# Sorting edges inside a graph network kernel: two products a bucket, names split into a power of two and a share, one-hots in batches of four

## The reference

```python
src, dst = ...                         # 41250 edges, both ends and self loops
xs = x[:, :C] @ W_in2f_s; xv = x[:, C:] @ W_in2f_v     # the table, from layernorm(x)
sj, vj = xs[idx_j], xv[idx_j]          # gathered by edge
W = (shifted_softplus(f_ij @ Wf1 + bf1) @ Wf2 + bf2) * rcut_ij[:, None]
x_ij = products of sj, vj, W and the edge's direction
agg = jax.ops.segment_sum(x_ij, idx_i, num_segments=n)
...
x = x + graph_layer(layernorm(x), ...)
x = x + experts(layernorm(x), ...)     # top-k tokens of 8 experts
```

## Time and profile before

| | us |
|---|---|
| median of 3 runs | 1451.07 (1449.11 to 1451.34) |
| the profiled execution | 1450.21 |
| its span | 1448.2 |
| last product of a column ends, about | 166.7 |
| first product of the loop starts | 178.4 |

### The profile page before, as it was taken

How to read it: one execution, slowest core, us unless ns; L and a number is a source line. 1 busy time by engine, 2 the same in 40 slices (tenths; PEclk the granted TensorE clock), 3 DMA queues, 4 the chain that set the end, 5 groups by cost and what they waited for, 6 DMA issues and landing times. The chain is left out here.

```text
span 1448.2 us, 26881 instructions
## 1 busy us (share of the span) xinstructions
PE 1336.5 (92%) x7095; PEld 786.7 (54%) x7095; DVE 1034.6 (71%) x2533; ACT 830.7 (57%) x2124; POOL 791.2 (55%) x834
## 2 busy tenths in 40 slices
PE   6888699999999999999999999999972699999997
PEld 1463356555555555555655555555561455555553
DVE  6998679989999899899999999999776311111110
ACT  5589777777777777777777777777551011111111
POOL 3147577777777777777777777777300122222211
PEclk7699889999999999999999999999995799999998
DMA  7135044444444444445443444434452155555521
GB/s 245 74 131 161 4 112 113 125 127 124 128 124 113 123 129 123 129 123 143 124 113 110 112 112 111 113 109 115 68 186 72 58 163 163 162 162 157 149 37 18
DMA packets 65872, 172.46 MB, mean 119 GB/s; under 512 B 14260, under 2 KB 22820, under 8 KB 65191
## 3 DMA queue, kind: packets, MB, share of 16 engines
q0 software_dynamic: 43424, 105.53, 28.2%
q1 hardware_dynamic: 22398, 66.38, 13.5%
HBM read 148.53 MB, written 18.08 MB: 115 GB/s over the span
## 5 line engine op out<-in xcount | busy, mean ns | idle before, releaser
L1114 PE MATMUL PS<-prod,oneh 128*64 128x256 f32 x2052 | 469.5, 382 | 6.4 <-DVE region_s L929 3.6
L562 POOL DMA_INDIRECT recs<-rec_d,inv_i x342 | 323.5, 946 | 117.2 <-issue 85.8
L573 POOL DMA_INDIRECT gath<-table_d,recs x342 | 324.1, 948 | 106.2 <-issue 77.1
L1114 PEld LDWEIGHTS PS<-prod,oneh 128*64 128x64 f32 x2052 | 268.5, 137 | 202.2 <-issue 80.3
L697 ACT ACTIVATE oneh<-oneh,recs 128x64 f32<-128x64 f32 x1026 | 282.2, 337 | 151.9 <-DVE oneh L906 150.6
L1107 PE MATMUL PS<-prod,oneh 128*64 128x256 f32 x1368 | 356.0, 392 | 0.0
L1095 PE MATMUL PS<-wf_sb,h_t 128*128 128x512 f32 x684 | 333.0, 609 | 2.9 <-DVE h_t L892 2.9
L917 DVE TENSOR_TENSOR prod<-PS,gath 128x768 f32<-128x768 f32 x342 | 323.3, 945 | 0.0
L929 DVE TENSOR_TENSOR region_s<-region_s,PS 128x512 f32 x342 | 231.7, 677 | 22.5 <-issue 16.7
L704 ACT COPY PS<-c_rep 128x512 f32<-128x512 f32 x338 | 190.7, 584 | 74.9 <-DVE prod L917 73.5
L1095 PEld LDWEIGHTS PS<-wf_sb,h_t 128*128 128x128 f32 x684 | 117.1, 191 | 118.9 <-issue 115.6
(11 more groups left out here) (262 smaller groups left out, 1520.8 us busy)
## 6 DMA issues: line engine op xcount, KB each, us to landing
region_r<-wu SPq DMA_DIRECT2D x16, 512.0 KB, 4.1
region_r<-wd SPq DMA_DIRECT2D x16, 512.0 KB, 5.6
region_u<-wu SPq DMA_DIRECT2D x16, 512.0 KB, 4.2
region_u<-wd SPq DMA_DIRECT2D x16, 512.0 KB, 5.4
recs<-rec_d,inv_i POOLq DMA_INDIRECT x342
gath<-table_d,recs POOLq DMA_INDIRECT x342, 3.3
region_u<-rec_in SPq DMA_DIRECT2D x1, 5168.0 KB, 21.7
rec_d<-region_u SPq DMA_DIRECT2D x1, 5168.0 KB
```

What stands on the lines that cost most here:

```text
L562: nc.gpsimd.indirect_dma_start(out=recs[:, q % RING, k, :], out_offset=None, in_=rec_d, in_offset=bass.IndirectOffsetOnAxis(ap=inv_i[:, t: ...
L573: nc.gpsimd.indirect_dma_start(out=gath[:, t % GRING, :], out_offset=None, in_=table_d, in_offset=bass.IndirectOffsetOnAxis(ap=recs[:, q % ...
L1114: return nc.tensor.matmul(to, oneh[:, slot, 1 + i, :], prod[:, slot, P_Q:P_B + i + 1:1 + i, :], start=i == 0, stop=i == 2, skip_group_chec ...
```

## The change

- `rec_in` is loaded ahead of the weights and x, x last. POOL does `lengths` before `weights`; ACT takes that root ahead of its work on x, and DVE the reciprocal in the middle of the buckets.
- The two halves of a column's start lie in one operand of 52 rows (`column_parts`), so a bucket takes two products. `row_of` gets a second copy of its rows, by a second ACT instruction.
- A name is a power of two that depends on the column, put on the tile one-hot as a constant (`weight(n)`), times a share that depends on the row alone, put on the slot one-hot (`share`). So ACT's Relu has the same operands for every column, and does four at once, 128x512, into a ring of its own of 16 (`scalar_oh`). The distances' ring holds two batches. There are 152 such columns (38 batches): four in nine up to column 143 and five in nine behind it (`LATE`). POOL has 61, from column 48 on.
- `node_variance` stands behind column 18, `node_scales` behind column 24, and two batches' distances and one Relu ahead of the normalising.
- The seeds stand behind the last column.
- `read_names` runs over the first 24 tiles and then over the rest, and POOL's gather of tile 24 waits for the second.

```diff
+LATE = 144
+BATCH = 4
+SCALAR_RING = 16
...
 def by_scalar(n):
-    return n >= ALONE and n % 9 % 2 == 1
+    return n >= ALONE and n % 9 in ((1, 3, 5, 7) if n < LATE else (1, 3, 5, 7, 8))
 def by_pool(n):
-    return n >= 8 * BESIDE and n % 9 in (4, 8)
+    return n >= 2 * ALONE and n % 9 in (0, 4)
...
-FAR = 4
+FAR = 2
+def weight(n):
+    return math.ldexp(-1.0 if n >= HALF else 1.0, LEAST + n % HALF - 127)
+FIRST = 24
...
                 sp.dma_start(src_i, src).then_inc(s_src, 16)
-                for cut in CUTS:
-                    sp.dma_start(x_sb[cut], x.rearrange("(p t) h -> p t h", t=BLOCKS)[cut]).then_inc(s_x, 16)
+                sp.dma_start(unsorted, rec_in).then_inc(s_edges, 16)
...
                     sp.dma_start(to, of).then_inc(s_small, 16)
-                sp.dma_start(unsorted, rec_in).then_inc(s_edges, 16)
+                for cut in CUTS:
+                    sp.dma_start(x_sb[cut], x.rearrange("(p t) h -> p t h", t=BLOCKS)[cut]).then_inc(s_x, 16)
...
-                    pool.wait_ge(s_rt, 2)
+                    pool.wait_ge(s_rt, 1)
...
+                lengths()
                 weights()
-                lengths()
                 directions()
                 constants()
...
+                        nc.gpsimd.tensor_scalar(slot_oh[:, n % OH_RING, :], iota_h[:, 0:P], bucket[:, n:n + 1],
+                                                share[:, 0:1], ALU.is_equal, ALU.mult).then_inc(i_hot, 1)
...
+                    if t == FIRST:
+                        hold(pool, i_ready, 2, pool_passed)
...
-                def distance(m):
-
-                    j = column(TURNS[m])
-                    if m == 0:
+                def distances(b):
+
+                    if b == 0:
                         act.wait_ge(i_name, 1)
...
+                    if b >= FAR:
+                        act.wait_ge(i_slot, b - FAR + 1)
+                    for m, n in list(enumerate(TURNS))[BATCH * b:BATCH * (b + 1)]:
+                        last = nc.scalar.activation(far[:, m % (FAR * BATCH), :], iota_h[:, 0:P], ACT.Abs,
+                                                    bias=bucket[:, n:n + 1], scale=-1.0)
+                    last.then_inc(i_far, 1)
+
+                def slot_one_hots(b):
+
+                    act.wait_ge(i_far, b + 1)
+                    first, last = BATCH * b, min(BATCH * (b + 1), len(TURNS))
+                    if last > SCALAR_RING:
+                        act.wait_ge(i_done, TURNS[last - 1 - SCALAR_RING] + 1)
+                    at, of = first % SCALAR_RING, first % (FAR * BATCH)
+                    nc.scalar.activation(scalar_oh[:, at:at + last - first, :], far[:, of:of + last - first, :], ACT.Relu,
+                                         bias=share[:, 0:1], scale=share[:, 1:2]).then_inc(i_slot, 1)
+
+                def slot_batches(first, last):
+                    for b in range(first, last):
+                        distances(b)
+                        if b >= 1:
+                            slot_one_hots(b - 1)
+
+                act.wait_ge(s_row, 2)
+                for at in (0, REC):
+                    nc.scalar.copy(row_of[at:at + BUCKETS], ident[at:at + BUCKETS, at:at + BUCKETS].unsqueeze(2).to_broadcast(
+                        [BUCKETS, BUCKETS, P])).then_inc(s_row, 1)
+                act.wait_ge(s_sq, 1)
+                nc.scalar.activation(squares[:, 0, :], squares[:, 3, :], ACT.Sqrt).then_inc(s_rt, 1)
                 act.wait_ge(s_x, 16 * len(CUTS))
...
+                slot_batches(0, 2)
                 act.wait_ge(s_norm, 1)
...
-                act.wait_ge(s_sq, 1)
-                nc.scalar.activation(squares[:, 0, :], squares[:, 3, :], ACT.Sqrt).then_inc(s_rt, 1)
+                def batches_of(n):
+                    return min(-(-sum(m < n for m in TURNS) // BATCH) + 1, BATCHES)
+
+                done = 2
                 for t in range(BLOCKS):
                     at = ALONE + BESIDE * t
-                    slot_columns(at, at + BESIDE // 2)
+                    slot_batches(done, max(done, batches_of(at + BESIDE // 2)))
+                    done = max(done, batches_of(at + BESIDE // 2))
                     evacuate_table(t)
                     if t + 2 < BLOCKS:
                         evacuate_x(t + 2)
-                    slot_columns(at + BESIDE // 2, at + BESIDE)
-                slot_columns(ALONE + BESIDE * BLOCKS, NCOLS)
+                    slot_batches(done, max(done, batches_of(at + BESIDE)))
+                    done = max(done, batches_of(at + BESIDE))
+                slot_batches(done, BATCHES)
+                slot_one_hots(BATCHES - 1)
...
                     for b in range(BUCKETS):
+                        if b == BUCKETS // 2:
+                            dve.wait_ge(s_rt, 1)
+                            nc.vector.reciprocal(squares[:, 1, :], squares[:, 0, :]).then_inc(s_recip, 1)
                         dve.wait_ge(s_pick, b + 1)
...
-                    slot, j = n % OH_RING, column(n)
+                    slot = n % OH_RING
                     if n >= OH_RING:
                         dve.wait_ge(i_done, n - OH_RING + 1)
-                    last = nc.vector.tensor_scalar(tile_oh[:, slot, :], iota_h[:, 0:TILES], target[:, j:j + 1], None,
-                                                   ALU.is_equal)
+                    last = nc.vector.tensor_scalar(tile_oh[:, slot, :], iota_h[:, 0:TILES], target[:, n:n + 1], weight(n),
+                                                   ALU.is_equal, ALU.mult)
                     if not by_scalar(n) and not by_pool(n):
-                        last = nc.vector.tensor_scalar(slot_oh[:, slot, :], iota_h[:, 0:P], bucket[:, j:j + 1],
-                                                       name[:, j:j + 1], ALU.is_equal, ALU.mult)
+                        last = nc.vector.tensor_scalar(slot_oh[:, slot, :], iota_h[:, 0:P], bucket[:, n:n + 1],
+                                                       share[:, 0:1], ALU.is_equal, ALU.mult)
                     last.then_inc(i_oh, 1)
...
+                def read_names(a, b):
...
+                link(nc.vector.memset(row_of, 0.0))
+                dve.sem_inc(s_row, 1)
+                link(nc.vector.memset(column_parts, 0.0))
...
-                node_variance()
 
                 for j in range(NCOLS):
                     column_one_hots(j)
-                    if j == ALONE // 3:
+                    if j == ALONE - 6:
+                        node_variance()
+                    if j == ALONE:
                         node_scales()
-                    if j == ALONE + BESIDE:
-                        dve.wait_ge(s_rt, 2)
-                        nc.vector.reciprocal(squares[:, 1, :], squares[:, 0, :]).then_inc(s_recip, 1)
                 dve.wait_ge(s_mapped, 1)
                 link(nc.vector.tensor_scalar(map_i[:, :], ps_map, BUCKETS - 1.0, float(HID), ALU.min, ALU.mult))
...
-                read_names()
-                dve.sem_inc(i_ready, 1)
+                read_names(0, FIRST)
+                read_names(FIRST, TILES)
...
-                    nc.tensor.matmul(to, row_of[:, b, :], column_low, start=False, stop=False)
-                    nc.tensor.matmul(to, row_of[:, b, :], column_high, start=False, stop=True).then_inc(s_pick, 1)
+                    nc.tensor.matmul(to, row_of[:, b, :], column_parts, start=False, stop=True).then_inc(s_pick, 1)
...
+                    slots = slot_oh[:, slot, :]
                     if by_scalar(n):
-                        pe.wait_ge(i_slot, scalars_until(n) + 1)
+                        m = TURNS.index(n)
+                        pe.wait_ge(i_slot, m // BATCH + 1)
+                        slots = scalar_oh[:, m % SCALAR_RING, :]
                     if by_pool(n):
                         pe.wait_ge(i_hot, OFFERED.index(n) + 1)
-                    nc.tensor.matmul(ps_inv, slot_oh[:, slot, :], tile_oh[:, slot, :], start=n == 0, stop=n == NCOLS - 1
+                    nc.tensor.matmul(ps_inv, slots, tile_oh[:, slot, :], start=n == 0, stop=n == NCOLS - 1
...
+                for j in range(ALONE + BESIDE * BLOCKS, NCOLS):
+                    add_column(j)
                 pe.wait_ge(s_wready, 2)
                 nc.tensor.matmul(ps_d, ones[0:1, :], c_sb[:, :], start=True, stop=True).then_inc(s_cps, 1)
                 for bank in ps_w:
                     nc.tensor.matmul(bank, ones[0:1, :], c_sb[:, :], start=True, stop=True).then_inc(seeded, 1)
-
-                for j in range(ALONE + BESIDE * BLOCKS, NCOLS):
-                    add_column(j)
                 pe.wait_ge(s_cps, 5)
 
```

89 lines of the change are left out of this document (29 added, 60 removed).

## The result

| | before | after |
|---|---|---|
| median of 5 runs | 1451.07 us | 1442.35 us |
| lowest to highest | 1449.11 to 1452.51 | 1440.54 to 1444.12 |
| span of the profiled execution | 1448.2 | 1440.5 |

The ratio is 0.9943, with a 95% interval of 0.9932 to 0.9953: 8 us faster, and clear of the scatter of the runs. The forecast was 1442.5 us. The total came out as said, but not by the steps as said, so the stages are read one by one. I count the loop over the tiles from PE's first product of it to the start of DVE's first product for the last tile (L915, after the change L930): it takes 861.2 us before and 859.1 after, so in the trace before it ends at 1039.6 and not at about 1085. The work behind it takes 408.6 and 408.1 us. So what the change does is looked for ahead of the loop, by comparing the starts of stages.

The account below looks back on a forecast made before the run. ACT was taken to bound the last columns, PE and ACT together the table stage, PE the buckets. Terms -0.8 + 2.2 + 6.6 + 0.6 = 8.6 us off the median 1451.07 gave 1442.5, range 1436 to 1447.5.

Parts of the forecast that it names:

- Buckets: Buckets and loads ahead of the columns: one product fewer saves about 4.7 us; columns start at 36.0 instead of 39.2.
- First block: Start of the first table block on PE: at 57.2 against 56.4, a loss of 0.8 us.
- x decides: At the first table block: x's load, sums and normalising set its start, so the early columns gain nothing there.
- Table stage: Ten turns between PE and ACT: 54 us, with 1.4 for half clock, against 56.2; gain 2.2 us.
- batches shorten ACT's work without shortening the loop that binds: In the table stage: the mean turn stays at 5.2 us, the old turn at full clock.
- Last stage: Last columns: ACT still binds, DVE 5 us behind; columns end at 158.7 instead of 166.7; 6.6 us in the sum.
- Into the loop: From last column to the loop over the tiles: L1086 at +11.1 instead of +11.7, gain 0.6 us.
- The rival of half clock at the seeds: Behind the last column: PE's clock drops, L1086 comes at +13.9, 2.2 us later than before; 1445.3 us; chance 0.18.
- Locks: Last stage: POOL's one-hots hold DVE up; wholly 1466 us, chance 0.04; half 1450.2, chance 0.03.
- the dearer tile one-hot: DVE's two-operation one-hot costs more: half rate 1443 to 1449.8 us, chance 0.06; one element a cycle 1491, chance 0.03.

Follow-up runs that it names:

- e4: The changed kernel with a third product, of zeros, for each bucket; ratio 0.9959 to the kernel before.
- e7: The changed kernel with the two loads of x issued straight behind the records' load, ahead of the weights; ratio 0.9958 to the kernel before.
- e5: The changed kernel again, unedited, on an experiment chip; ratio 0.9953 to the kernel before.
- e10: The kernel before with only the seeds moved behind the last column; ratio 0.9990 to the kernel before.
- e2: The changed kernel with ACT's larger share in the last stage taken back (LATE = 323 instead of 144); ratio 0.9945 to the kernel before.
- e3: The changed kernel with the seeds moved back between the table stage and the last columns; ratio 0.9958 to the kernel before.
- e1: The changed kernel with ACT making slot one-hots for twelve columns more ahead of its evacuations; ratio 0.9861 to the kernel before.
- e9: The kernel before again, unedited, with its own trace on an experiment chip; ratio 1.0003 to the kernel before.
- e6: The changed kernel with ACT's one-hots twelve columns further ahead and the seeds between table stage and last columns; ratio 0.9879 to the kernel before.

## Why the prediction was right, point by point

*Buckets.* Right: a product costs 0.22 (e4) to 0.26 (1.03 less 0.77), columns at 36.65 and 36.21 against 36.0. The records landed earlier than charged (POOL starts at 17.45, not 19.5), DVE came to the reciprocal later (24.95, not 24). `directions` cost 1.3 to 1.7 of the 2 us charged.

*First block.* 57.54 and 57.09 for 57.2, but "x decides" was wrong, and the prediction's own numbers said so: ACT's sums at 43.1, DVE's nineteenth column at 44.4. Measured 44.1 and 45.05. e4 moved DVE alone and the block went with it, one for one. e7 brought x 2 us earlier, but made DVE later by the lock, and the block went with DVE. Of the 4.5 us that the saved product brings at the first column, 4.5 reach the first block, and 1.1 reached the loop in e4, the rest being lost or won by the clock of two turns.

*Table stage.* This is the step that failed, in a term of the sum: half clock, charged at 1.4 us. The turns at full clock were a little shorter than said (5.75, 3.95 and 5.32; predicted 5.95, 4.3 and 5.45), and the last has no transposes. Nine of them would take 44.6. The prediction's nine, from the first block at 57.2 to the tenth at 105.8 (the stage's end at 111.2 less one turn), take 48.6 with its half clock in. They took 51.7 in the first trace and 50.1 in e5, so half clock cost 7.1 and 5.5. The kernel before had half clock in this stage too: the granted clock of its nine turns was 0.87 in both its traces, and 0.96 in e10, whose edit lies behind them; with the new preparation it was 0.83 (the first trace), 0.88 (e5), 0.85 (e2) and 0.88 (e3). The nine turns of the kernel before took 51.0 and 51.3, so the stage gained nothing where 2.2 were promised. And "batches shorten ACT's work without shortening the loop that binds" took the loop for given; e1 shows that the binding was an order of issue, worth 12 us.

*Last stage.* Right in all its terms: batches at 2.00 measured 2.01, the Relu of 512 at 0.80, the last part 53.1 (predicted 158.7 minus the tenth block at 105.8, 52.9) against 59.2. DVE behind by 5, measured 6.4, and e2 confirms both bounds. No run takes the batches out alone; but with ACT's share of 133 columns as before, e2 still has a last part of 51.1 for 59.2, so the gain is that of the batches, with POOL's 61 columns instead of 50. The last column was at 162.3 in the first trace, 3.6 later than forecast, 3.4 of it from the table stage.

*Into the loop.* 11.0 for 11.1. The rival of half clock at the seeds, to which I gave 0.18, happened in three of the eight traces with seeds at the end (e1, e2, e10), for 0.8 to 2.2 us. It did not happen in either trace of the changed kernel.

*The sum.* Split at the tenth block and at the last column, the forecast was 1.7 + 6.3 + 0.6 = 8.6 us. The first pair of traces gives -1.7 + 6.1 + 0.7 = 5.1, the second (e9 and e5) 1.2 + 6.1 + 0.8 = 8.0 (with rounding); the ratios over all runs give 8.3 and 7.9. So the last two terms are what the change brings, each time, and the first scatters by 3 us with the turns that fall into half clock. Its mean is near nothing: the tenth block starts at 107.5, 108.4 and 105.5 in the three traces with the old preparation up to there (before, e9, e10) and at 109.2, 107.2, 107.2 and 106.7 in the four with the new one (after, e5, e2, e3). That leaves some 6.3 us (6.1 + 0.7 and the means' -0.5) to the preparation, and 1.6 to 2.0 of the 7.9 and 8.3 us in the times outside of what the stages show. The 2.1 us inside the loop of the first pair were not seen again and are of the size by which loops differ within one group (2.0, 5.5 and 6.1 us). That scatter is the likelier reading; that nothing of it belongs to the change isn't shown. The mechanism of the last stage was right, but that the total came out within 0.2 us of 1442.5 is in part luck: on the mean the first term was some 2 us too good, and a gain of about the same size came that no term of the sum had.

*Locks and the dearer tile one-hot* did not come: the tile one-hot L852 with two operations takes 309 ns on the mean, 344 wide, like L839's 0.30 to 0.31 with one, and DVE made its last one-hot of a column at 155.65, which leaves no room for POOL's 33 one-hots of 0.95 us to hold it up.

## What to carry to other kernels

Where two engines go round a loop in step and both show idle time, look at what each has issued ahead of the instruction it waits at; one or two batches moved ahead of one wait gave 12 us here, more than the whole change. Price what the lower clock may take in a stage with waits from several turns and several traces, since it moved this stage's end by 3 us between kernels with the same program up to there. Before an edit moves work past a ring, compute the slack of every engine that feeds the ring, and price the moved work at the lower clock too: the same eight seeds in the same place took 3.59 us and cost the columns nothing in e6, and took 6.70 and cost them 2.9 in e3.

## What the hardware showed that was not expected

The clock fell inside the table stage behind waits of PE, but not behind each. In the first trace of the changed kernel each of the three waits of 1.64 us for ACT was followed by a block at half clock, which cost that turn 1.6 us; in e5 two of the three such turns were, in e4 none, though there the block behind a wait of 1.2 us was. In e1, where PE doesn't wait there, the granted clock was 1.00 from 70 us to 140, close to the last column. It also fell under the seeds, in which PE has no wait: the eight took 3.59 us at a clock of 1.00 in e6, 4.03 at 0.88 in the kernel before and 6.70 at 0.53 in e3.

The changed kernel's loop took 859 us in the first trace and 1081 in e5, and that of the kernel before 861 and 1061 (e9), with the start of the loop and the tail equal within 2 us. Windows of the changed kernel over the same 100 us, first trace and e5:

```profile
600.00:700.00 100.00, 99.62 (x561) 58.24 (x560) 91.50 (x181) 72.98 (x191) 75.63 (x80) 1.00 0.44 127
```

```profile
600.00:700.00 100.00, 85.52 (x453) 47.03 (x454) 74.39 (x147) 56.96 (x152) 59.94 (x64) 0.98 0.35 98
```

The clock is nearly the same and POOL issues 64 gathers instead of 80; the DMA engines are less busy, not more. Whether it is the chip or its state at the time, and why, isn't settled: the chip of the first traces isn't on record, and no experiment was made on it.

A load issued 13.5 us earlier, straight behind one of 5.3 MB, landed 2 us earlier (e7), and the weights behind it landed 10 us later.
